# Shared experts' second half in 256-token pieces inside the routed loops, through one PSUM bank

## What is computed

```python
# stage A: 8 routed experts of width 128, top 2 of 8, and shared experts (width 256)
y_all = einsum('etm,emh->eth', leaky(x @ w_gate[e]) * (x @ w_up[e]), w_down)
y = (y_sel * topk_w).sum(1)
p = leaky(x @ sw_gate) * (x @ sw_up) @ sw_down          # shared, every token
yA = y + p
# stage B: 8 routed experts of width 512 (gelu), top 2; no shared experts
# stage C: multi-query attention with bias, 16 heads, layer norms
# stage D: 16 routed experts of width 128 (silu, biases), top 2, and shared experts
hs = silu(xf @ sw1.T + sb1) * (xf @ sw3.T + sb3)
out = x + C + routed + (hs @ sw2.T + sb2)
```

## Time and profile before

| | before |
|---|---|
| median of three runs | 890.14 us (889.52 to 890.62) |
| profiled execution, its own time | 891.04 us |
| span inside it | 889.3 us |
| busy: PE, DVE, POOL, ACT | 785.1, 461.3, 456.1, 377.1 us |
| granted TensorE clock, mean | 0.953 |

### The profile page before, as it was taken

One profiled execution on the slowest core, in us unless ns is written; L12 is line 12 of the kernel. 1 busy time (PEld: TensorE's weight loads), 2 busy tenths in 40 slices (PEclk: granted clock), 3 DMA queues, 4 the chain that ended last, 5 costly groups with the idle time before them and its releaser, 6 DMA issues.

```text
span 889.3 us, 16732 instructions
## 1 busy us (share of the span) xinstructions
PE 785.1 (88%) x4252; PEld 543.2 (61%) x4253; DVE 461.3 (52%) x1561; ACT 377.1 (42%) x1174; POOL 456.1 (51%) x522
## 2 busy tenths in 40 slices
PE   7868988937999999879999999999999997898891
PEld 3446755824666676647776776767777445675551
DVE  0873434675222222246657566666756387464446
ACT  3323432303333333146656666666666542243330
POOL 1377776006626542254756566475654126777750
PEclk9999999757999999979999999999999999899996
DMA  7863333724544120194010101011000002333346
GB/s 273 320 238 107 102 104 108 222 93 151 175 150 140 60 65 30 60 365 192 1 31 8 37 0 36 0 36 36 0 12 2 24 0 79 107 101 100 104 137 214
DMA packets 45098, 89.41 MB, mean 101 GB/s; under 512 B 7728, under 2 KB 34864, under 8 KB 43504
## 3 DMA queue, kind: packets, MB, share of 16 engines
q1 hardware_dynamic: 30736, 43.80, 14.4%
q0 software_dynamic: 12000, 32.78, 11.9%
q10 hardware_dynamic: 2304, 12.14, 3.5%
HBM read 66.02 MB, written 22.68 MB: 100 GB/s over the span
## 4 chain that ended last, share of the span: by engine, by line
PE 57%; POOL 12%; DVE 11%; DMA 8%; issue 8%; SPq 2%; ACT 2%; DVEq 0%; POOLq 0%; ACTq 0%
PE psH L663 10%; POOL work L958 5%; PE psY L1026 5%; PE psY L680 5%; PE psM L1079 5%; PE psH L1045 5%; PE psM L680 4%; PE psL L1068 4%; PE psHT L1055 4%; POOL d_pairs L966 3%; PE psHT L672 2%; DVE work L890 2%; PE psH L488 2%; PE psY L1031 2%; POOL a_pairs L966 2%
## 5 line engine op out<-in xcount | busy, mean ns | idle before, releaser
L1400 POOL TENSOR_TENSOR work<-work,region_ac 128x386 f32<-128x386 f32 x128 | 119.6, 945 | 91.5 <-ACT work L1152 45.9
L663 PE MATMUL psH<-region_bd,work 128*128 x344 | 126.2, 491 | 0.3 <-ACT work L724 0.3
L1167 ACT ACTIVATE work<-work 128x129 f32<-128x129 f32 (+1 forms) x256 | 114.1, 448 | 11.0 <-DVE work L1262 11.0
L1262 DVE CUSTOM_DVE_ANT_0 work<-psH,work 128x129 f32<-128x129 f32 (+1 forms) x256 | 79.5, 347 | 3.5 <-PE psH L1045 3.5
L771 DVE TENSOR_TENSOR work<-psH,region_bd 128x256 f32<-128x256 f32 (+1 forms) x86 | 46.8, 544 | 64.4 <-PE psH L663 58.1
L966 POOL DMA_INDIRECT b_pairs<-work,home x39 | 37.7, 967 | 74.9 <-DVE work L790 68.1
L663 PEld LDWEIGHTS psH<-region_bd,work 128*128 128x128 f32 x344 | 61.0, 197 | 22.9 <-issue 19.9
L672 PE MATMUL psHT<-ident,work 128*128 128x128 f32 x242 | 49.8, 285 | 24.7 <-DVE work L778 13.9
L672 PEld LDWEIGHTS psHT<-ident,work 128*128 128x128 f32 x242 | 31.7, 141 | 64.6 <-DVE work L778 23.1
L958 POOL DMA_INDIRECT work<-y_scratch,inv x39 | 37.6, 965 | 63.7 <-DVE inv L897 52.1
L1026 PE MATMUL psY<-work,region_ac 128*128 128x256 f32 x256 | 66.8, 384 | 0.5 <-ACT work L1161 0.5
(11 more groups left out here) (225 smaller groups left out, 1612.3 us busy)
## 6 DMA issues: line engine op xcount, KB each, us to landing
region_bd<-in_b_w ACTq DMA_DIRECT2D x2, 4096.0 KB, 21.0
work<-a_pairs SPq DMA_DIRECT2D x16, 256.0 KB, 3.8
work<-b_pairs SPq DMA_DIRECT2D x16, 256.0 KB, 2.9
region_bd<-in_d_w SPq DMA_DIRECT2D x1, 4096.0 KB, 14.7
region_bd<-in_d_b SPq DMA_DIRECT2D x2, 2048.0 KB, 25.5
work<-d_pairs SPq DMA_DIRECT2D x16, 256.0 KB, 3.8
acc<-in_x SPq DMA_DIRECT2D x4, 512.0 KB, 4.6
region_ac<-in_a_gu SPq DMA_DIRECT2D x1, 2048.0 KB, 11.7
```

Of the source, the lines that this page charges most:

```text
L663: last = pe.matmul(psH[:, h, 0:f.hw], xT[:, h, k, :], f.w_in(k, e), start=(k == 0), stop=(k == KD - 1))
L1167: nc.scalar.activation(c_p[:, o, a:z], c_sc[:, o, a:z], ACT.Exp, scale=-1.0, bias=c_min[:, o, i:i + 1], accum_out=c_sum[:, j % 2, o, i:i + ...
L1400: pool.tensor_tensor(c_bm[:, 2 * (j % 2) + o, :], c_mp, c_bias[:, 2 * j + o, :], ALU.subtract).then_inc(C.bm_ready, 1)
```

## The change

The shared experts' units that are left when the routed loop starts are done inside that loop. In A four units are left (4 to 7; before, two were left), in D two (6 and 7). They are cut into pieces of 256 tokens: gate and up of a piece fit side by side in one PSUM bank. That bank is the second one of `psHT`; the routed loops of A and D turn their inner rows in the first one alone. A has eight pieces, behind tiles 0, 2, ... 14, D four, behind tiles 3, 6, 9 and 12. Token tile outputs 8 to 15 go through the same bank, behind slot tiles 32 to 39 in A and 40 to 47 in D. In A, DVE makes the inner rows of every piece (three instructions); in D, ACT does the silu and DVE one instruction. D's residual adds for token tiles 8 to 15 move into the slot loop as well. A's units 5 to 7 no longer use DVE behind the routing, and unit 4 no longer ACT and POOL ahead of it. ACT's and DVE's loops in A and D are unrolled like PE's: tiles 0 to 15 written out, 8 per round after that.

```diff
+        a_first = ((0, None), (1, None), (2, 0), (3, 1))
+        d_first = ((0, None), (1, None), (2, 0), (3, None), (4, 1), (5, None))
+        a_fill = Fill({2 * j: (4 + j // 2, j % 2) for j in range(8)}, A.NT - 7)
+        d_fill = Fill({3 + 3 * j: (6 + j // 2, j % 2) for j in range(4)}, D.NT - 7)
+            hT_banks = ffn_hT[:1] if st.shared_fills else ffn_hT
...
+        def pe_fill(pe, sh, tile):
+            if tile in sh.fill.pieces:
+                q, c, at, before = piece_of(sh, tile)
+                pe.wait_ge(sh.h_ready, len(sh.first) + before)
+                tokens = slice(q * QUAD * P + at.start, q * QUAD * P + at.stop)
+                for n in range(2):
+                    w = (n * CHUNKS + c) * P
+                    for k in range(KD):
+                        last = pe.matmul(fill_gate_up[:, n, :], sh.w_in[:, k, w:w + P], sh.xT[:, k, tokens],
+                                         start=(n == 0 and k == 0), stop=(k == KD - 1), skip_group_check=True)
+                last.then_inc(sh.h_mm, 1)
+            t = sh.fill.out_of(tile)
+            if t is not None:
+                q, i = divmod(t, QUAD)
+                pe.wait_ge(sh.h_ready, len(sh.first) + len(sh.fill.order))
+                pe.wait_ge(sh.y_out, t)
+                for c in range(CHUNKS):
+                    last = pe.matmul(fill_y, sh.hT[:, q % 2, c, i * P:(i + 1) * P], sh.w_out[:, c, :],
+                                     start=(c == 0), stop=(c == CHUNKS - 1))
+                last.then_inc(sh.y_mm, 1)
...
+        def dve_fill(dve, sh, kind, tile):
+            if tile - 1 in sh.fill.pieces:
...
+                dve.wait_ge(sh.y_mm, QUAD * (q - 1))
+                if kind == "leaky":
...
+                    nc.vector.tensor_scalar(act_gate, gate, 0.01, None, ALU.mult).then_inc(sh.h_leaky, 1)
...
+                    nc.vector.tensor_tensor(act_gate, act_gate, gate, ALU.max).then_inc(sh.h_leaky, 1)
...
+                    nc.vector.tensor_tensor(hidden, act_gate, up, ALU.mult).then_inc(sh.h_ready, 1)
...
+            t = sh.fill.out_of(tile - 1)
+            if t is not None and sh is D.shared:
+                add_x(dve, t)
...
-            pe.wait_ge(fA.y_out, A.NT)
-            pe_shared_rest(pe, A.shared)
...
-            pe.wait_ge(fD.y_out, D.NT)
-            pe_shared_rest(pe, D.shared)
```

More of the change, by code:

```diff
@@ L125, in __init__, with out_of @@
         self.y_out = sem(f"{name}_y_out")
+class Fill:
+    def __init__(self, pieces, first_out):
+        self.pieces, self.first_out = pieces, first_out
+        self.order = sorted(pieces)
+    def out_of(self, tile):
+        return tile - self.first_out + TT // 2 if 0 <= tile - self.first_out < TT // 2 else None
 class Shared:
-    def __init__(self, sem, name, kept, xT, hT, parts, w_in, w_out, b_in, by_vector):
+    def __init__(self, sem, name, kept, xT, hT, parts, w_in, w_out, b_in, by_vector, first, fill):
         self.xT, self.hT, self.parts, self.w_in, self.w_out, self.b_in = xT, hT, parts, w_in, w_out, b_in
+        self.first, self.fill = first, fill
         self.kept = kept
@@ L541, in pe_shared_in, with piece_of @@
             last.then_inc(sh.h_mm, 1)
+        def piece_of(sh, tile):
+            i, half = sh.fill.pieces[tile]
+            return i // CHUNKS, i % CHUNKS, slice(half * DIM, half * DIM + DIM), sh.fill.order.index(tile)
+        def pe_fill(pe, sh, tile):
[18 more added lines that the diff above has]
+                last.then_inc(sh.y_mm, 1)
         def pe_shared_out(pe, sh, q):
@@ L555, in pe_route_and_shared @@
         def pe_route_and_shared(pe, st):
-            sh = st.shared
+            sh, n = st.shared, len(st.shared.first)
             pe_shared_in(pe, sh, 0)
@@ L587, in act_shared, with act_fill @@
                         nc.scalar.copy(acc[:, t, :], shared_y[t % 2]).then_inc(sh.y_out, 1)
+        def act_fill(act, sh, kind, tile):
+            if tile - 1 in sh.fill.pieces and kind != "leaky":
+                q, c, at, before = piece_of(sh, tile - 1)
+                act.wait_ge(sh.h_mm, len(sh.first) + before + 1)
+                act.wait_ge(sh.h_ready, len(sh.first) + before)
+                nc.scalar.activation(sh.parts[:, c, 0, at], fill_gate_up[:, 0, :], ACT.Silu, bias=sh.b_in[:, c:c + 1]
+                                     ).then_inc(sh.part_ready, 1)
+            t = sh.fill.out_of(tile)
+            if t is not None:
+                act.wait_ge(sh.y_mm, t + 1)
+                nc.scalar.copy(acc[:, t, :], fill_y).then_inc(sh.y_out, 1)
         def act_shared_in(act, sh, i, kind):
@@ L677, in body @@
                     pe.wait_ge(f.hT_ready, t + 1)
-                    wait(pe, f.y_out, t - 1)
+                    wait(pe, f.y_out, t + 1 - len(f.y_banks))
                     for j in range(f.hk):
-                        last = pe.matmul(ffn_y[h], hT[:, h, j * P:(j + 1) * P], f.w_out(j, e),
+                        last = pe.matmul(f.y_banks[h % len(f.y_banks)], hT[:, h, j * P:(j + 1) * P], f.w_out(j, e),
                                          start=(j == 0), stop=(j == f.hk - 1))
                     last.then_inc(f.y_mm, 1)
+                if f.st.shared_fills and isinstance(s0, int):
+                    pe_fill(pe, f.st.shared, s0 + u)
             experts.fetch(0, 0)
@@ L745, in body @@
                     wait(act, f.y_mm, t - 1)
-                    nc.scalar.copy(hT[:, h, 0:f.hk * P], psHT[:, h, 0:f.hk * P]).then_inc(f.hT_ready, 1)
+                    nc.scalar.copy(hT[:, h, 0:f.hk * P], f.hT_banks[h % len(f.hT_banks)][:, 0:f.hk * P]).then_inc(f.hT_ready, 1)
+                if f.st.shared_fills and isinstance(s0, int):
+                    act_fill(act, f.st.shared, f.kind, s0 + u)
             copy_x(0, 0)
-            steps(act, f.n, body, 1, 2)
+            steps(act, f.n, body, 1, 2, *f.unrolled)
         def dve_ffn(dve, f):
@@ L1677, in _ @@
             pe.wait_ge(D.shared.y_out, tiles_first)
[L1678 removed]
+            pe.wait_ge(D.shared.h_ready, len(d_first))
             pe_ffn(pe, fD)
[L1680 to L1681 removed]
         @block.vector
@@ L1712, in _ @@
             dve.wait_ge(D.weights_loaded, D.loads)
-            dve_shared(dve, D.shared, "silu", shared_first)
-            def add_x(first, last):
-                for t in range(first, last):
-                    dve.wait_ge(D.shared.y_out, t + 1)
-                    nc.vector.tensor_tensor(acc[:, t, :], acc[:, t, :], x2[:, t, :], ALU.add).then_inc(C.base_ready, 1)
+            dve_shared(dve, D.shared, "silu", d_first)
             def combine_d(s0, u, t):
```

90 lines of the change are left out of this document (49 added, 41 removed).

## The result

| | before | after |
|---|---|---|
| median (20 runs each) | 889.82 us | 892.68 us |
| ratio, 95% interval | | 1.0032 (1.0022 to 1.0042) |
| profiled execution, its span | 891.04, 889.3 us | 893.22, 891.4 us |

The account below looks back on a forecast made before the run. The prediction took POOL to set the pace, with PE slower only in runs of scatters. A's +2.6 and D's +3.4 summed to +6.0: 891.04 to 897.0 us profiled, 896.1 as median, range 886.5 to 901.

Parts of the forecast that it names:

- Part 1: Routing list of A: without unit 4 on POOL, the list is ready and POOL's first gather starts earlier, -2.1 us.
- Part 2: Start of A's loop: PE starts at about 55.1 instead of 63.24, which is only lead, no gain by itself.
- Part 3: Eight pieces in A: DVE frees the bank late, two tiles take 5.85 us, scatter 13 starts at 103.5; +4.8 us.
- second rival: Only the outputs cost, pieces are absorbed in both loops (4.9 us for two tiles in A): 889.5 us; 22%.
- Part 4: Single psHT bank: PE's turn waits for a copy it needed anyway, 0 us.
- Part 5: Eight outputs in A: five fall in the run of scatters, less PE's 1.2 us of lead, +3.1 us.
- Part 6: Behind A's loop: rests leave, so the first combination and token tile 4 come sooner after the last scatter, -3.2 us.
- Parts 7 to 9: All of D: pieces +1.8, outputs +3.6, adds and collision leaving the combination at the end -2.0; +3.4 us.
- part 7: Four pieces in D: the one of tile 12 stands in the run of scatters and costs PE, ACT and DVE time, +1.8 us.
- part 8: Eight outputs in D: two hide, six cost PE 0.86 us each, less half a microsecond and the last copy's lead, +3.6 us.
- B and C follow unchanged: Stages B and C, between A and D, take the same time as before and add nothing to the sum.
- first rival: All of it hides: pieces and outputs cost POOL nothing, leaving -2.1, -3.2 and -2.0, so 882.8 us; 10%.

Follow-up runs that it names:

- e3: The changed kernel with DVE's and ACT's instructions of a piece moved from the end of the next body to its beginning; 889.46 us, ratio 0.9993.
- e5: e3 with the outputs eight tiles earlier, behind slot tiles 24 to 31 in A and 32 to 39 in D; 889.69 us, ratio 1.0002.
- e7: e5 with the pieces behind tiles 0 to 7 in A and 0 to 3 in D; 889.55 us, ratio 0.9999.
- j1: e7 with DVE's loop in A written out as in the change; 885.75 us, ratio 0.9964.
- e8: The changed kernel with only the eight outputs eight tiles earlier in both loops; 892.09 us, ratio 1.0031.
- e6: The kernel before with only ACT's and DVE's loops of A written out, no work moved; 886.87 us, ratio 0.9975.
- the padded kernels: The kernel before with one-column memsets on DVE at the start: 152 (C's code at 533), ratios 1.0025, 1.0021; 102 (at 483), 0.9981, 0.9978, 0.9997.
- j2: The kernel before with 102 one-column memsets on DVE at the start; 889.27 us, ratio 0.9997.
- e1: The kernel before with the change in A alone, D as before; 891.30 us, ratio 1.0014.
- i2: The kernel before with 102 one-column memsets on DVE at the start, on one of the two slower chips; ratio 0.9978.

## Why the prediction was right and wrong

- *Part 1, -2.1:* -2.0 (52.62 to 50.64), and -1.7 to -2.5 over all twenty profiles when counted from PE's first result. Right.
- *Part 2, the loop's start:* only lead, as said; PE starts at 57.2 and not at 55.1; 1.46 us of that it waits for the rows of tile 0.
- *Part 3, +4.8:* scatter 13 at 103.77 (forecast 103.5), +4.9 behind the first gather. Right, and for the reason given: e3 removes the wait for the bank by moving DVE's instructions alone. e3's cycle, 4.98, all but meets the second rival's condition (4.9 us for two tiles). Scatter 13 was not on time for all that: in e3, e5, e7 and j1 the pieces still cost 1.4 to 3.2 us instead of 4.9.
- *Part 4:* no wait seen there. Right.
- *Part 5, +3.1:* +2.2; the last scatter of A starts at 155.71 (forecast 156.4). I had taken PE's lead as the 1.2 us of the last copy. But copy 38 had itself waited 0.58 us for a DMA, so PE was further ahead than its copies showed. That would be two thirds of what is missing; no run tried it.
- *Part 6, -3.2:* -2.2 (30.85 to 28.68 from last scatter to last combination). Over-sized by 1.0: the first combination does come 5.4 us behind the last scatter, 2.8 sooner, and token tile 4 comes at 166.41, 3.25 sooner behind that scatter. But DVE now waits for the loads (0.95 us ahead of token tile 4), and on the tiles behind it 1.1 us of the gain are lost again.
- *A:* +2.8 (203.67 to 206.49 at B's first gather). Forecast +2.6.
- *Parts 7 to 9:* +1.2, +2.65 and -1.9 against +1.8, +3.6 and -2.0; D +1.95 instead of +3.4, the second step that was off. In e3 and e5, with the pieces first on DVE and ACT, the way to scatter 13 is 48.93 and 48.60 against before's 48.49: most of part 7's 1.2 is where their instructions stand, and the 1.72 that I charged for PE's matmuls is nearly all hidden. The early outputs of e5 and e8 give part 8 back in full, so its cause is right and PE's lead was again taken too small. The trace of before had the sign of it: copy 42 still waited for a DMA, four copies later than the copy 38 that I went by.

```profile
851.48 0.42 DVE L790 TENSOR_TENSOR work<-psY,region_bd 128x256 f32<-128x256 f32 x1 [0.92 <-DMA d_pairs<-work,home]
```

- ***"B and C follow unchanged"*** is the step that failed. B does (+2.9 at its end). C's work is unchanged, but its code stands elsewhere in DVE's program, and that is -2.7 us, a term that I had put at nothing. e6 shows it without the change's work, and the padded kernels show that the place alone moves C. The sum with it and with the measured sizes is +2.9 - 2.7 + 1.95 = +2.1, the difference of the two spans. Of the 3.9 us between +6.0 and +2.1, C is 2.7 and D 1.5; A and B together go 0.3 the other way.
- *The first rival* needed other places for the pieces and outputs. The Trainium skill, "Perfetto Trace Analysis", section "Optimization Strategy", says that interleaving may help where the most contended engine changes. The change does not bear it out (+2.9 us). A in e5, e7 and j1 does: it is 1.5 to 4 us shorter than where it is unchanged, part 1's 2.1 among them. The outputs cost nothing in e7, e8 and j1, where POOL alternates gathers and scatters (49.7 to 50.0 from scatter 13 to 38), and 2.2 in a run of scatters.

How the code's place acts is open. One pair of profiles suggests the packets of an instruction queue. While SP's load of `b_pairs` at 464.35 (467.64 after) is on its way, the kernel before has such a packet, and the load lands 3.9 us after its issue (median); after, there is none, and it takes 2.9. Before:

```profile
q8 instruction: 1, 0.02, 1.1%
work<-b_pairs SPq DMA_DIRECT2D x2, 256.0 KB, 3.9
```

After:

```profile
q1 hardware_dynamic: 684, 0.65, 54.8%
work<-b_pairs SPq DMA_DIRECT2D x2, 256.0 KB, 2.9
```

The other profiles speak against it. j1, whose C is short (364.26), has the packet beside that load (issued at 461.46) and a landing of 3.7:

```profile
q8 instruction: 1, 0.02, 1.5%
work<-b_pairs SPq DMA_DIRECT2D x2, 256.0 KB, 3.7
```

So have e6 and j2 (3.5 and 3.7), while e5, with the longest C, has 3.4. Nor is it the length of DVE's copy on which PE waits: 412 ns on average before and 369 after, but 358 in e5.

```profile
L1274 DVE COPY region_bd<-work 128x256 f32<-128x256 f32 x62 | 25.5, 412 | 0.0
```

```profile
L1359 DVE COPY region_bd<-work 128x256 f32<-128x256 f32 x63 | 23.2, 369 | 0.0
```

What DVE lacks when it stands still, and what makes a batch longer with 381 than with 502, no run here shows.

## What to carry to other kernels

In this kernel work of the idle engine had to go where the pace-setting engine's list alternates, not where its cheapest items stand in a row. Look for such runs before you place a filler, and try the filler ahead of, not behind, what the pace-setter waits for (e3: 889.46 against 892.68). A change that makes one engine's program longer can move a later stage by a few microseconds without touching its work: cut every profile at the same landmarks, compare the stages that should be equal, and repeat the change's code length without its work before you explain a total or claim a gain.

## What the runs showed of the hardware

- The place of a loop's code in DVE's program moves five batches of stage C from 190.0 to 196.0 us in twenty profiles, on all the chips tried. At the worst place, 533, DVE stands idle twice for 1.7 to 2.0 us with no releaser.
- A wait of PE at the start of A's loop left the granted clock of the stretch from 55 to 65 us at 1.00 in some executions (waits of 1.33 us in e8 and 1.46 in the changed kernel) and at 0.81 to 0.83 in others (1.37 in e3, 1.54 in e1); the first piece then takes 1.89 or 2.73 to 3.00 us. The length of the wait does not part the two.
- Two chips ran the same kernel in 962 instead of 890 us. C took there what it takes elsewhere (i2 364.45); the loss lies in the routed loops (59.5 us instead of 48.2 up to scatter 13, B 179.7 instead of 167.1), where PE stands idle with no releaser. From the waits of A in i2, columns: engine, line, releaser, us, times, longest:

```profile
PEld psH L663 <- issue: 10.3, 5, 2.5
...
PE psH L663 <- issue: 6.7, 4, 2.1
PEld psHT L672 <- issue: 6.5, 3, 2.8
```

What these chips are short of was not tried.
